# Routed experts of a GNN and MoE kernel: other places for a tile's output and for GpSimd's gather

## The reference, cut to what matters

```
x = x + gnn(layernorm(x), ...)                  # message passing over 50000 edges, 3125 nodes of 256 features
u = layernorm(x)
shared = gelu(u @ W1s + b1s) @ W2s + b2s        # 256 -> 1024 -> 256
w, i   = top_k(softmax(u @ Wr), 2)              # 8 experts, two per node, w normalised to sum 1
h      = gelu(einsum('sd,edf->sef', u, W1p) + b1p)
priv   = einsum('sef,efd->sed', h, W2p) + b2p
x = x + shared + sum over the two chosen experts of w * priv[expert]
```

## Time and profile before

| what | us |
|---|---|
| median of 3 runs | 1309.96 |
| the profiled execution, its own time | 1312.32 |
| its span (first to last instruction) | 1310.3 |
| TensorE's busy time | 1198.2 (91%) |
| VectorE | 1002.2 (76%) |
| ScalarE | 828.7 (63%) |
| GpSimd | 772.8 (59%) |
| mean granted clock of TensorE | 0.957 |

### The profile page before, as it was taken

The page is one execution under the profiler, slowest core; times in us unless marked ns, Lnnn a source line. Parts: engine busy times, 40 slices in busy tenths (PEclk is TensorE's granted clock), DMA queues, the critical chain, the costliest instruction groups (busy, mean ns, idle before and its releaser), DMA issues. The chain is left out here.

```text
span 1310.3 us, 31820 instructions
## 1 busy us (share of the span) xinstructions
PE 1198.2 (91%) x8631; PEld 1107.6 (85%) x8631; DVE 1002.2 (76%) x2523; ACT 828.7 (63%) x2353; POOL 772.8 (59%) x873
## 2 busy tenths in 40 slices
PE   2879999999999999999978889999799999999991
PEld 1669998888888888888867769999799999999991
DVE  7589999999999999999966767544466666665651
ACT  2678888888888888888854565544344444434430
POOL 7167888778887888878852102552245555555552
PEclk9979999999999999999997879999899999999996
DMA  6433333333333333333435462331424434433222
GB/s 239 164 99 99 95 97 97 91 99 96 93 99 95 94 99 95 94 95 96 119 99 178 162 230 91 106 95 51 142 45 109 102 79 110 97 84 74 45 45 25
DMA packets 81050, 135.08 MB, mean 103 GB/s; under 512 B 16190, under 2 KB 56174, under 8 KB 80480
## 3 DMA queue, kind: packets, MB, share of 16 engines
q0 software_dynamic: 31792, 67.29, 21.0%
q1 hardware_dynamic: 45280, 63.66, 14.9%
q10 hardware_dynamic: 3920, 3.41, 0.8%
HBM read 104.73 MB, written 29.57 MB: 102 GB/s over the span
## 5 line engine op out<-in xcount | busy, mean ns | idle before, releaser
L552 POOL DMA_INDIRECT rows<-h_tab,src_st x392 | 402.4, 1027 | 120.0 <-issue 120.0
L576 ACT ACTIVATE hots<-hot,sh_st 128x128 f32<-128x128 f32 x1568 | 467.9, 390 | 2.8 <-PE psY L743 1.7
L743 PEld LDWEIGHTS psY<-prod,hots 128*128 128x128 f32 x2352 | 324.1, 191 | 20.3
L743 PE MATMUL psY<-prod,hots 128*128 128x128 f32 x2352 | 325.6, 275 | 0.0
L740 PE MATMUL psY<-prod,hots 128*128 128x256 f32 x784 | 234.1, 380 | 0.0
L1766 ACT ACTIVATE q_hf<-q_psA,x_b 128x256 f32<-128x256 f32 x232 | 110.0, 474 | 192.0 <-PE q_psA L1311 189.7
L636 DVE TENSOR_TENSOR prod<-psW,rows 128x384 f32<-128x384 f32 x392 | 213.8, 545 | 0.0
L1711 POOL DMA_INDIRECT out_rows<-q_ob,q_index x58 | 119.3, 2057 | 134.8 <-DMA out_rows<-q_ob,q_index 86.3
L1311 PE MATMUL q_psA<-q_xhi,x_whi 128*128 x464 | 133.4, 287 | 7.8 <-DVE q_xlo L1804 7.8
L651 DVE TENSOR_TENSOR y_sb<-y_sb,psY 64x512 f32 x196 | 133.5, 681 | 7.5 <-issue 4.4
L1897 PE MATMUL q_psB<-x_whi,q_hhi 128*128 128x256 f32 x464 | 132.9, 286 | 0.1
(11 more groups left out here) (216 smaller groups left out, 2565.0 us busy)
## 6 DMA issues: line engine op xcount, KB each, us to landing
x_raw<-in_w SPq DMA_DIRECT2D x18, 1024.0 KB, 5.7
cols_lo<-ele_split SPq DMA_DIRECT2D x196, 32.0 KB
rows<-h_tab,src_st POOLq DMA_INDIRECT x392, 2.7
x_sb<-in_x SPq DMA_DIRECT2D x5, 640.0 KB, 5.7
h_tab<-x_sb ACTq DMA_DIRECT2D x5, 640.0 KB, 3.3
u_x<-in_x SPq DMA_DIRECT2D x5, 640.0 KB, 7.2
xnew_d<-u_x SPq DMA_DIRECT2D x5, 640.0 KB, 3.4
xn_d<-u_xn SPq DMA_DIRECT2D x5, 640.0 KB, 4.8
```

The source lines that it names most:

```text
L552: pool.indirect_dma_start(out=rows[p][:, c, :, :].rearrange("p a u -> p (a u)"), out_offset=None, in_=h_tab, in_offset=bass.IndirectOffset ...
L576: ins = nc.scalar.activation(hots[p][:, 4 * c + k, :], hot[p][:, c, :], ACT.Copy, scale=sh_st[p][:, 4 * c + k:4 * c + k + 1])
L743: ins = nc.tensor.matmul(y[:, 2 * k::6 - 2 * k, :][:, 0:2, :], hots[p][:, 4 * c + k + 1, :], a[:, 0::k + 1, :][:, 0:2, :], start=False, st ...
```

## The change

In VectorE's queue, for the last expert alone, each `output` is moved forward by about one place: the output of tile 25 comes at the end of tile 26 (f = 7, `late`), that of tile 26 in tile 27 at f = 1, that of tile 27 in tile 28 at f = 1 (`early`), and that of tile 28 is behind the last tile as before. Up to tile 24 nothing moves.

In GpSimd's queue, for all tiles, the order becomes `add(d, 0)`, `rows_of(d + 4)`, `landed(d, 0)`, `add(d, 1)`, `landed(d, 1)`. The number of instructions, transfers and bytes is the same.

```diff
             rows_of(4)
             pool.wait_ge(v["o_out"], 16 * NG)
-            add(0, 0)
-            landed(0, 0)
-            add(0, 1)
-            with pool.Fori(1, all_but_two) as d:
-                rows_of(within(d + 4, TILES + 1))
-                landed(d - 1, 1)
+            def adds(d, gather=None):
                 add(d, 0)
+                if gather is not None:
+                    rows_of(gather)
                 landed(d, 0)
                 add(d, 1)
+                landed(d, 1)
+
+            adds(0)
+            with pool.Fori(1, all_but_two) as d:
+                adds(d, within(d + 4, TILES + 1))
             for d in range(2):
-                landed(all_but_two + (d - 1), 1)
-                add(all_but_two + d, 0)
-                landed(all_but_two + d, 0)
-                add(all_but_two + d, 1)
-            landed(all_but_two + 1, 1)
+                adds(all_but_two + d)
...
-            def tile(s, e, done=None, after=None):
+            def tile(s, e, done=None, after=None, early=None, late=None):
...
                     if f == 0 and done is not None:
                         output(*done)
+                    if f == 1 and early is not None:
+                        output(*early)
+                    if f == FC - 1 and late is not None:
+                        output(*late)
                     if f == 2:
                         split_x(s + 1)
...
+                last = e == EXPERTS - 1
                 tile(within(first + 1), e, (within(first + 1), e - 1) if e > 0 else None,
-                     split_w1 if e + 1 < EXPERTS else None)
+                     None if last else split_w1, late=(within(first + 2), e) if last else None)
                 dve.sem_inc(begun, 1)
-                further(dve, n, first, lambda s, e=e: tile(s, e, (s, e)))
-            output(first + n, EXPERTS - 1)
+                further(dve, n, first, lambda s, e=e, last=last:
+                        tile(s, e, None if last else (s, e), early=(within(s + 1, TILES), e) if last else None))
             output(first + n + 1, EXPERTS - 1)
```

## The result

The changed kernel took 1337.28 us (median of 4 runs, 1332.4 to 1344.54), the one before 1312.43 beside it (4 runs): ratio 1.02, 95% interval 1.0119 to 1.0281. It is slower, by 25 us. Each ratio is formed from the fast runs alone and each median from all runs, so the two differ where a kernel also had slow runs, as in experiment 7. The forecast of 1328 had the sign and the place; it was 9 too low, inside its own range of 1318 to 1340.

What follows compares the result with a forecast made beforehand. GpSimd's queue was taken as the pacemaker, 12.37 us a cycle against TensorE's 11.81. 21 cycles of +0.69 (+14.5) - 1.5 + 2.8 + 2 = +17.8 on the profiled 1312.3: 1330, median 1328; overall range 1305 to 1344, own range 1318 to 1340.

Steps and rivals of the forecast that it cites:

- Part 1: GpSimd's queue: the gather, not the first landing, sets a tile's second scatter-add, 3.82 after the first's issue: +0.59 per cycle.
- Part 2: Gather now beside VectorE's busiest stretch: one of two gathers takes 1.30, not 0.95; +0.3 per cycle, bounds 0 and 1.09.
- short scatter-adds: Rival, 10%: VectorE's work thins out, the first scatter-add's issue falls from 2.66 to 1.6; faster, 1299 or 1300.
- a fall of A0's issue time: Sign of being wrong: the issue time of a tile's first scatter-add, mean 2.66, falls.
- Part 3: GpSimd, second scatter-add to the next tile's first, now without a gather: near 6.2, -0.2 per cycle, bounds 0 and -0.4.
- The rows that arrive late: Rival, 9%: transpose-to-transpose loop through the gather, 11.8, or 14.0 with a late load; 12 tiles pay up to 1.0: 1340.
- Part 4: Start of the paced stretch: a landing no longer stands behind a gather waiting for a transpose; -1.5 once, bounds 0 and -2.5.
- Parts 5 and 6: Last expert: TensorE stands some 9 us, tile 26's second scatter-add comes +2.8 later; lower clock after that stand, +2.
- No price: Rival, 20%: the gather is hidden as well as before, so its new place costs nothing; 1311.
- The port: Rival, 14%: gathers beside VectorE's dense work grow as the first scatter-add does, +1.09 per cycle; 1344.

Runs made afterwards that it cites:

- experiment 7: Third chip, against kernel before: changed kernel 1.0237; GpSimd's order alone 1.025; changed without tile 30's gather 1.0197; bias ahead of release wait, earlier last-expert outputs, no tile-30 gather 0.9923.
- experiment 5: Changed kernel with the gather's two index copies moved ahead of the tile's first scatter-add: 1324.73 us, ratio 1.0101 to the kernel before.
- experiment 3: Changed kernel without the gather for tile 30: 1339.72 us, ratio 1.0207 to the kernel before.
- after_no30_b: Changed kernel without the gather for tile 30, run on a third chip: 1395.41 us, ratio 1.0197 to the kernel before.

## Why the prediction was right, and where not

**Part 1, the gather ahead of the landing: right.** In the 13 cycles of the changed kernel with a short A0 (1.57 to 1.94), the best are 5.39 from A0 to A1, 1.57 + 3.82, the forecast's number.

**Part 2, the dense stretch: the step that was mis-sized.** The prediction took +0.3 a cycle, for one stretched gather, and left the stretch of the copies out of its sum. From the end of A0's issue to A1 it grew by 1.30 (3.19 to 4.49), not by 0.89: 0.63 for the place (3.19 to the 3.82 of part 1, whose 3.23 was a little over the mean before), 0.59 for the copies (0.89 to 1.48), 0.06 for two gathers. The remaining 0.02 is not assigned. The gathers' mean of 1.03 meets the letter of the forecast ("over 1.0") and not its size. The bounds of part 2 held it, 0 to 1.09, but they were bounds on gathers; the earlier trace rows leaves the copies' line out, and it was the one to ask about. The cycles come in two kinds, worked out from the timeline's rows:

| | cycles | A0 to A1 | A1 to A0 | sum |
|---|---|---|---|---|
| before, A0 long (3.2) | 12 | 6.38 | 6.60 | 12.98 |
| before, A0 short | 9 | 5.14 | 6.42 | 11.56 |
| after, A0 long (3.2) | 7 | 8.60 | 6.16 | 14.76 |
| after, A0 short (one 2.60) | 14 | 5.72 | 7.13 | 12.86 |

Where A0 is long after the change, so are the copies: 2.14 to 3.56 behind the seven long ones, 0.87 to 1.23 behind the others. VectorE's timeline beside the pair of 2.14 above:

```profile
1075.20 0.68 DVE L1856 TENSOR_TENSOR x_wlo<-x_raw,x_whi 128x512 fp32r<-128x512 f32 x1
1075.80 0.29 DVE L1808 CAST q_hhi<-q_hf 128x256 fp32r<-128x256 f32 x1
1076.00 0.42 DVE L1812 TENSOR_TENSOR q_hlo<-q_hf,q_hhi 128x256 fp32r<-128x256 f32 x1
1076.33 0.69 DVE L1856 TENSOR_TENSOR x_wlo<-x_raw,x_whi 128x512 fp32r<-128x512 f32 x1
...
1077.14 0.42 DVE L1812 TENSOR_TENSOR q_hlo<-q_hf,q_hhi 128x256 fp32r<-128x256 f32 x1
```

VectorE runs subtractions with two SBUF inputs one behind the other, the weight splits (L1856) among them. That they are what stretches GpSimd fits these rows, and experiment 5 shows that the place decides and not the instruction. The two timelines of the kernel before, laid side by side, sort the cases further: VectorE splits weights beside all 12 long A0s from tile 3 to 23 and beside none of the 9 short ones (1.62 to 1.99), and in the last expert, which has no next weights to split, no A0 from tile 25 on takes over 1.66. But this is no proof: no run took VectorE's work away alone.

The Trainium skill, page "SBUF — State Buffer", section "SBUF: two separate sides", names a port pair that the two engines share and that whichever starts first holds for its whole instruction: a GpSimd operation, or, among others, one of VectorE's with two SBUF inputs against a GpSimd operation that reads SBUF. It adds that GpSimd can't write a transfer's descriptors meanwhile. The trace agrees in direction for A0 (1.58 to 3.18), for a gather right behind it (0.98 to 1.97) and for plain 128x1 copies.

**What the forecast left out, in the other direction.** A0's issue fell from 2.66 to 2.19, since only 7 of 21 are long and not 12. That is -0.47 a cycle, the first half of the rival "short scatter-adds". The prediction's last line named a fall of A0's issue time as a sign of being wrong. The sign came true and the forecast still held: the fall did outweigh the +0.39 of parts 1 and 3, but it did not reach the rival's 1.06, and the copies' +0.59, which neither had, was larger. So the total came as near as it did because a gain that was left out stood against a loss that was too small; that is luck.

**Part 3, A1 to the next A0: right for 16 cycles, wrong for 5.** (Before, 5 of the 21 were 6.9 to 7.2, not 4 as the prediction counted; its -0.2 doesn't hang on that.) The 16 are 6.04 to 6.76, mean 6.31 (forecast 6.2 to 6.3). The other five are 7.56 to 9.42 and turn the mean, forecast at -0.2, to +0.29 (6.52 to 6.81). In three VectorE waited for the release, because A1 had landed late (it lands 3.8 after its start at best). The chain of waits in order of time, and VectorE's output behind it:

```profile
1124.08 3.83 DMA out_rows<-q_ob,q_index
...
1135.81 6.11 DMA out_rows<-q_ob,q_index
```

```profile
1142.20 0.15 DVE L1822 COPY q_index<-x_meta_all 128x1 int32 x1 [0.47 <-POOLq L1718]
```

A1 now is issued 0.30 behind a gather whose data are still on the way. Without the loads one such cycle remained (7.95), so the loads account for part. In the other two VectorE did not wait for a release; it was TensorE that was late:

```profile
988.45 1.12 PE L1884 MATMUL q_psX<-ident,x_slot_rows 128*128 128x128 f32 x4 [3.03 <-DMA x_slot_rows<-xn_d,x_slot_index]
1003.02 0.60 PE L1884 MATMUL q_psX<-ident,x_slot_rows 128*128 128x128 f32 x4
```

```profile
985.00:990.00 5.00, 1.97 (x11) 1.76 (x10) 1.46 (x6) 0.77 (x3) 1.62 (x1) 0.77 0.53 133
990.00:995.00 5.00, 5.00 (x27) 5.00 (x27) 2.46 (x7) 2.15 (x5) 2.91 (x4) 0.55 0.23 26
995.00:1000.00 5.00, 5.00 (x45) 5.00 (x44) 4.04 (x11) 2.12 (x5) 3.12 (x3) 1.00 0.38 66
```

TensorE stood for rows until 988.45, its granted clock fell to 0.55, near the lower of its two levels, and the tile took 14.57 from transpose to transpose and not 11.81. The output at 1004.33 came right behind the transpose. The other slow tile is the one from 1219.75 to 1233.19, 13.44 long behind a stand of 2.24, with a granted clock of 0.68 from 1218 to 1223.

**The sum of the cycles.** +1.30 - 0.47 + 0.29 = +1.12, times 21 = +23.4, where the forecast had +0.69 and +14.5. In us over the stretch: place 13.2, copies 12.3, gathers and the unassigned rest 1.7, shorter A0s -9.9, three late landings 6.2, two slow tiles of TensorE 4.4 (both against the mean of 6.31), and the 6.31 itself against the 6.52 before, 21 times, -4.4.

**The rows that arrive late: underrated.** The prediction had TensorE slip once, at no cost, and gave the rival 9%. TensorE stood for rows in 9 tiles of the stretch, 21.1 us, once for 5.04. In a cycle with a long A0 the loop through the gather is as long as GpSimd's own: A0 at 1114.45, transpose at 1126.47 (12.02), output at 1128.11 (1.64), A0 at 1130.16 (2.05), together 15.71. The rival had 11.8 for it and 14.0 with a late load; the copies and the landing of 2.7 are what it lacked. The output waited 5.50 us for the release in that same cycle, so this stand cost little by itself. What the stands cost in the sum is the clock behind them, in the two cycles above.

**Part 4, the hold: the gain came and was lost again.** -1.5 was taken; the start came 0.7 later. A0(2) did come 1.1 sooner (976.79, not 977.87), but its issue took 3.17 and not 1.69, and the index copies behind it 2.15, the same price as in part 2.

**Parts 5 and 6, the last expert and the clock: right in the main.** The end grew by 5.5, forecast 4.8. TensorE stood at a down slice behind `low` in tile 28, 6.35 us (forecast 9), and for 5.06 once more behind the output of tile 27, where the prediction had the down slices done in time:

```profile
1298.61 0.58 PE L1900 MATMUL q_psB<-x_whi,q_hhi 128*128 128x256 f32 x1 [6.35 <-DVE q_hlo L1812]
...
1317.14 0.58 PE L1900 MATMUL q_psB<-x_whi,q_hhi 128*128 128x256 f32 x1 [5.06 <-DVE q_hlo L1812]
```

```profile
1298.61 1.58 POOL L1711 DMA_INDIRECT out_rows<-q_ob,q_index  x1 [5.02 <-DVE q_ob L1827]
1306.55 0.60 POOL L1625 COPY x_slot_index<-x_meta_all 128x1 int32 x2 [6.36 <-PE q_psX L1884]
...
1310.75 1.62 POOL L1711 DMA_INDIRECT out_rows<-q_ob,q_index  x1 [0.31 <-issue]
```

```profile
1295.00:1300.00 5.00, 1.39 (x6) 1.39 (x7) 3.47 (x13) 0.00 (x0) 1.39 (x1) 0.50 0.04 6
1300.00:1305.00 5.00, 5.00 (x38) 5.00 (x37) 1.65 (x6) 0.00 (x0) 0.19 (x1) 0.83 0.24 26
```

A0(26) to A1(26) is 12.1 (forecast 10.9): GpSimd waits 6.36 for the transpose of the slipped tile, at a clock of 0.50, then 0.83. What follows A1(26) took 29.1 us, where the prediction had it unchanged at 27.8. That this gather is the link is shown by the traces of experiment 3 and of after_no30_b, on two chips; the gain it would bring is not shown by their medians.

**The other rivals.** "No price" fell with the cycle of 13.49. "The port" had the mechanism nearly right and the victim wrong: it priced both gathers at +1.09, and the stretch cost 0.65 a cycle, nearly all of it on the copies. As the sum stands, the truth lies between the forecast and that rival.

## What to carry to other kernels

Moving work on an engine's queue from behind a wait to ahead of it saves only what of the wait is longer than the work, at the new place's durations. Price every instruction of the moved step, the small ones too, as they run beside what the neighbouring engine does there, and look at the instruction already there for a hint: here A0 ran at twice its length in that place, in 12 of 21 tiles, before anything was moved. When one step paces the rest, first take from the path between release and next issue whatever needs no release: here two additions moved over one wait brought the step down to TensorE's pace.

## What was not expected of the hardware

- Two plain copies of 128x1 int32 on GpSimd, together 0.30 to 0.43 us where VectorE had gaps between its operations, took 2.14 and up to 3.56 us beside its subtractions. The issue of a scatter-add takes one of few values there, 1.58 or 3.18, seldom 1.9 or 2.6.
- A scatter-add issued 0.30 us behind a gather landed 3.83 after its start in one tile, 5.18 and 6.11 in two others; three of 21 were late, and one of 21 without the weight loads.
- One gather, for tile 11, landed 6.82 us after its issue, where the median of the edge stage is 2.7.
- Behind a stand of 3 us at TensorE the granted clock was 0.55 for 5 us, and the tile was 2.8 us longer (14.57, not 11.81), with no other wait of TensorE in it.
